# Block numbers loaded four at a time, last stores not held back, and two steps of a hand-written order moved

## The reference, cut to what matters

```python
def _L0_ffn_ref(hidden_states, gate_weight, gate_up_proj, down_proj):
    NUM_EXPERTS, TOP_K, THRESHOLD, HIDDEN, INTER = 32, 8, 0.8, 256, 96
    x = hidden_states.reshape(-1, H)
    probs = softmax(x @ gate_weight.T)
    top_vals, top_idx = top_k(probs, TOP_K)
    renorm = top_vals / sum(top_vals)
    num_keep = minimum(sum(cumsum(renorm) < THRESHOLD) + 1, TOP_K)
    rw = top_vals * (arange(TOP_K) < num_keep);  rw = rw / sum(rw)
    combine = sum(one_hot(top_idx, NUM_EXPERTS) * rw[..., None], axis=1)
    for w_gu, w_d, ce in experts:          # a scan over the 32 experts
        g, u = split(x @ w_gu.T)
        out += (silu(g) * u) @ w_d.T * ce[:, None]

x = x + attention(layernorm(x))
x = x + cross_attention(layernorm(x), ctx)
x = x + _L0_ffn_ref(layernorm(x), ...)
```

## Time and profile before

| | |
|---|---|
| runs shown | 521.94 us median of 3 (520.2 to 522.55) |
| profiled execution | 522.98 us, its span 521.0 us, mean granted clock 0.97 |
| PE, DVE, POOL, ACT busy | 89%, 73%, 63%, 61% of the span |
| chain that ended last | PE 52%, DVE 18%, DMA 8%, issue 7%, SPq 7%, ACT 6% |

### The profile page before, as it was taken

One profiled execution on the slowest core, in us unless ns is written; L12 is line 12 of the kernel. 1 busy time (PEld: TensorE's weight loads), 2 busy tenths in 40 slices (PEclk: granted clock), 3 DMA queues, 4 the chain that ended last, 5 costly groups with the idle time before them and its releaser, 6 DMA issues.

```text
span 521.0 us, 12667 instructions
## 1 busy us (share of the span) xinstructions
PE 464.8 (89%) x3120; PEld 394.9 (76%) x3120; DVE 379.2 (73%) x1854; ACT 317.7 (61%) x869; POOL 327.0 (63%) x473
## 2 busy tenths in 40 slices
PE   3789999999999999999977999999999999798930
PEld 2577777788787778777757898889999999697820
DVE  4356788888877888887875886556556568988796
ACT  2367778787777777777843565556566565455520
POOL 4112257778777678776667667776676666574770
PEclk9989999999999999999987999999999999999985
DMA  6322446852223223221137569998655679988685
GB/s 196 95 111 75 164 128 211 239 161 91 93 97 103 103 92 115 80 99 72 73 121 227 177 220 297 302 294 281 200 147 162 194 220 336 337 281 311 220 294 182
DMA packets 52263, 93.80 MB, mean 180 GB/s; under 512 B 9975, under 2 KB 41247, under 8 KB 52003
## 3 DMA queue, kind: packets, MB, share of 16 engines
q1 hardware_dynamic: 37346, 46.11, 30.4%
q0 software_dynamic: 12240, 32.14, 16.5%
q10 hardware_dynamic: 2608, 14.76, 8.3%
HBM read 53.61 MB, written 43.41 MB: 186 GB/s over the span
## 4 chain that ended last, share of the span: by engine, by line
PE 52%; DVE 18%; DMA 8%; issue 7%; SPq 7%; ACT 6%; POOL 1%; POOLq 0%; ACTq 0%; DVEq 0%
PE bank L1406 11%; PE bank L1441 7%; DVE NM L788 6%; PE bank L1103 6%; PE bank L1244 4%; DVE NM L790 4%; PE bank L1361 4%; PE bank L1286 3%; SPq L360 3%; PE bank L1260 3%; DMA pool_a<-rows 3%; DMA qN<-rows 2%; SPq L365 2%; PE bank L1165 2%; PE bank L1431 2%
## 5 line engine op out<-in xcount | busy, mean ns | idle before, releaser
L468 POOL DMA_INDIRECT rows<-rowb,idx x112 | 110.8, 989 | 56.7 <-DVE rowb L888 28.3
L1406 PE MATMUL bank<-wgu_sb,PT 128*128 x572 | 108.6, 333 | 3.2 <-issue 3.2
L1406 PEld LDWEIGHTS bank<-wgu_sb,PT 128*128 128x128 f32 x572 | 93.3, 194 | 4.8 <-issue 4.4
L478 POOL DMA_INDIRECT parts<-PT,dst_all x72 | 71.5, 993 | 33.1 <-issue 23.8
L495 ACT ACTIVATE PT<-bank 128x512 f32<-128x512 f32 x108 | 61.2, 593 | 29.7 <-PE bank L1441 21.2
L1441 PE MATMUL bank<-wd_sb,VC 96*128 x286 | 75.0, 384 | 1.8 <-issue 1.3
L997 DVE SCALAR_TENSOR_TENSOR PT<-PT,bank 128x192 f32<-128x192 f32 x72 | 25.2, 350 | 53.4 <-ACT PT L622 53.4
L1441 PEld LDWEIGHTS bank<-wd_sb,VC 96*128 96x128 f32 x286 | 51.3, 189 | 9.8 <-issue 5.6
L588 ACT ACTIVATE PT<-bank 128x512 f32<-128x512 f32 x96 | 53.6, 619 | 4.6 <-PE bank L1260 4.5
L622 ACT ACTIVATE PT<-bank 128x192 f32<-128x192 f32 x72 | 23.8, 330 | 50.4 <-PE bank L1406 50.4
L495 ACT ACTIVATE Q<-bank 9x256 fp32r<-9x256 f32 (+1 forms) x96 | 42.5, 443 | 11.3 <-PE bank L1239 9.6
(11 more groups left out here) (270 smaller groups left out, 1148.7 us busy)
## 6 DMA issues: line engine op xcount, KB each, us to landing
pool_a<-rows SPq DMA_DIRECT2D x96, 148.5 KB
qN<-rows SPq DMA_DIRECT2D x47, 148.5 KB
wgu_sb<-wgu_d SPq DMA_DIRECT2D x8, 768.0 KB, 5.2
rows<-pad SPq DMA_DIRECT2D x33, 152.0 KB
pool_a<-parts ACTq DMA_DIRECT2D x5, 896.0 KB
KA<-parts ACTq DMA_DIRECT2D x5, 896.0 KB, 6.8
Q<-parts ACTq DMA_DIRECT2D x5, 896.0 KB
wd_sb<-wd_d SPq DMA_DIRECT2D x2, 1536.0 KB, 10.7
```

The costliest lines, as they stand in the source:

```text
L468: gp.indirect_dma_start(out=rows, out_offset=bass.IndirectOffsetOnAxis(ap=idx[b % 2][:, k:k + 1], axis=0), in_=rowb[b % 2][:, :], in_offse ...
L478: gp.indirect_dma_start(out=parts, out_offset=bass.IndirectOffsetOnAxis(ap=dst[q % NDST][:, j:j + 1], axis=0), in_=yb[q % FEED][:, j, :], ...
L1406: last = t.matmul(GU_PS[q % 2][:, j * 2 * NI:(j + 1) * 2 * NI], xTb[q % 2][:, j, k * P:(k + 1) * P], wgu_sb[:, k, one_of(expert[i]), :].sq ...
```

## The change

1. `choose` takes a pair instead of a pair and a block. For every second pair it loads four numbers into four registers (`pe.load`) and keeps each (`pe.snap`); before, each block had its own `value_load`. The 143 loads become 36. Their place moves from behind each block's gate and up product to the end of the down product of the pair before.
2. The second stores of pairs 48 to 67 no longer wait for `th`.
3. POOL's inverse root of the last tile gets sort key 48.4 instead of 51.3.
4. `la3` gets 87.8 instead of 86.2 on PE, and 88.2 instead of 86.5 on DVE.

```diff
+CLOSE = 48
-           "la2": 80 + (SEEN - 1) * PERIOD, "la3": 86.2 + (SEEN - 1) * PERIOD},
+           "la2": 80 + (SEEN - 1) * PERIOD, "la3": 87.8 + (SEEN - 1) * PERIOD},
...
-    "POOL": {"r17": 28.5, "wo": 51.3}}
+    "POOL": {"r17": 28.5, "wo": 48.4}}
...
-                    if j == 1 and DEEP <= q < NPAIR - 4:
+                    if j == 1 and DEEP <= q < CLOSE:
                         pool.wait_ge(S["th"], nth("th", q + 4))
...
+            four = [pe.alloc_register(f"expert{n}") for n in range(4)]
...
-            def choose(q, j):
-                i = 2 * q + j
-                if i == NA:
+            def choose(q):
+                if q >= NPAIR or q % 2:
+                    return
+                if 2 * q == NA:
                     pe.wait_ge(S["lists"], 4)
-                expert[i] = pe.value_load(tbl_i[0:1, i:i + 1], min_val=0, max_val=NE - 1)
+                pe.load(four, tbl_i[0:1, 2 * q:2 * q + 4])
+                for n in range(4):
+                    expert[2 * q + n] = pe.snap(four[n], min_val=0, max_val=NE - 1)
...
             def gates(q):
-                for j in range(2):
-                    if q < NPAIR and j < BLOCKS[q]:
-                        gu(q, j)
-                    if q + 1 < NPAIR and j < BLOCKS[q + 1]:
-                        choose(q + 1, j)
+                for j in range(BLOCKS[q] if q < NPAIR else 0):
+                    gu(q, j)
...
-                for q in range(2):
-                    for j in range(2):
-                        choose(q, j)
+                choose(0)
                 gu(0, 0)
                 gu(0, 1)
...
                     if q > 0:
                         dn(q - 1)
+                    choose(q + 2)
                     hT_(q)
...
                     gates(q + 2)
                     dn(q - 1)
+                    choose(q + 3)
```

More of the change, by code:

```diff
@@ L65 @@
            "po": 62.9, "g7": 64, "g8": 73.7, "g9": 74.2, "g10": 75.2, "g11": 75.4, "g12": 75.6, "g13": 75.8, "la1": 77.4 + (SEEN - 1) * PERIOD,
-           "la2": 83 + (SEEN - 1) * PERIOD, "la3": 86.5 + (SEEN - 1) * PERIOD},
+           "la2": 83 + (SEEN - 1) * PERIOD, "la3": 88.2 + (SEEN - 1) * PERIOD},
     "POOL": {"r1": -12, "r4": -2.2, "r7": 3.9, "r13": 17.4, "kL": 29.5, "r17": 46.3, "wo": 51.5, "xT": 60, "sc0": 74.6, "sc1": 77.4, "sc2": 80.5,
```

## The result

The changed kernel takes 513.93 us in the median of 4 runs (512.39 to 516.68). The kernel before, run beside it, takes 522.25. The ratio is 0.9846, 95% interval 0.9808 to 0.9885. The medians are 8.3 us apart; the forecast was 514.6 us, 7.3 less than before. The profiled execution took 512.39, span 510.5, mean granted clock 0.983 (before 522.98, 521.0, 0.97).

A forecast was written before the change was run, and what follows sets the result against it. PE bounds 346 to 424 us; the waits lie before and after. 4.4 - 0.8 + 0.8 + 0.5 + 2.9 - 0.5 + 0 = 7.3 us off 522.98 gives 515.7, as median 514.6; range 511.5 to 519.3, forecast's own 513 to 517.

The forecast's parts named there:

- First use, idle: PE at the list's first use: one load replaces four, first gate product 2.2 us earlier, bounds 1.9 to 2.5.
- The clock: PE behind the first use of the list: stays at 2.4 GHz after the shorter idle, 3.0 us gained, bounds 0 to 3.0.
- The root: POOL at the last tile: the move alone gives nothing; in the old place about 3 of 4.4 us would go.
- POOL's queue: POOL's scatters and stores after the head: delay DVE before pair 13, losing 1.0 to 2.7 us; 0.8 taken off.
- Loads in the pairs: PE after waits for rows: fewer loads give 0.8 us before 346 us and 0.5 later, bounds 0 to 2.5.
- Stores not held: Last stretch: POOL keeps up, last store 3.9 us earlier, gain 2.9 at the end; 0.5 off for delayed rows.
- The tail's sum: The end: 2.9 us gained, from 1.0, 0.2 of DVE's 0.83 and its 1.67 wait for the last fetch.
- The list's product: PE ahead of the list's product: waits for DVE's maxima either way, zero gain, bounds -0.3 to +0.5 us.
- The clock did not fall: Rival at the list's first use: the clock falls all the same, 516.9 us, chance 0.16.
- POOL's queue took nothing that reached the end: Rival: POOL's queue takes the head's gain, its 2.00 us idle at 305.46 stays, 517.3 us, chance 0.14.
- no row was crowded out: Rival after 430 us: stores crowd out rows, 10.4 us lost against 7.3 gained, 525.0 us, chance 0.12.
- The change does nothing at the end: Rival at the end: rows or sums, not stores, set DVE; tail gives 0.5, not 2.9; 517.0 us, chance 0.06.

The follow-up runs named there:

- three more edits: Changed kernel with ten destination buffers, the first list's product as before, and ACT's last copy ahead of tile 13's fetch: 513.26 us, 0.9825 of the kernel before.

## Why the prediction was right

The time, the sign and the forecast's own range (513 to 517) hold. By its steps:

- **First use, idle.** Forecast 2.2, measured 2.2 (2.94 to 0.75), since ACT's copy is late next. The load of four took 336 ns in the median. The Trainium skill, "Runtime: NRT & Kernel Launch", section "Instruction fetch mechanics", has 200 ns per register even in bulk, for loads from HBM. The trace doesn't agree for this table: 336 ns for four registers.
- **The clock.** Forecast that it stays full, for 3.0 us. It stayed in all 11 profiles with the short idle. But the 3.0 is a price of one execution: with the long idle it fell for 6.8 us, for 3.4 us and not at all in three profiles (pair 0 at 24.9, 24.0 and 21.8). The profile that the forecast was read from is the one with the longest fall, and that this size fits the medians is in part luck. Undoing the first use's load on top of the pairs' costs 2.9 us, give or take 2.6 (0.9979 - 0.9924): the idle's 2.2, and 0.7 for the rest.
- **The root.** Forecast: by itself nothing, without it 3 of 4.4 would go. The mechanism is shown on both sides: with the loads as before the new place, the list and the stores not held give 0.9979 together. The size was 4.5; in its profile the clock falls behind the wait that the old place leaves, 5.1 us by pair 4.
- **POOL's queue.** DVE's wait for pair 5's store grew from 1.64 to 2.76 us and ended at 316.88, which is 318.7 by the clock of the profile before; forecast was near 320. That it takes 0.8 us from the end isn't shown: with the waits gone, the time was the same. From pair 4 to pair 20 the lead did not fall (5.4 to 5.7).
- **Loads in the pairs.** Forecast 0.8 ahead of 346 us and 0.5 behind. This term was mis-sized: 3.2 us in all, and of that some 1.6 behind pair 16. I had counted five places and taken off what rows or DVE hide; in one profile five gaps of 1.75 us in all stand against a loss of 1.6.
- **Stores not held.** Forecast 2.9 less 0.5. The step that failed is "POOL idles 3.92 us for `th`", and with it "without the hold POOL keeps up". Only about 1.4 of the 3.92 us were the hold; the other 2.5 have another cause, which still makes a gap without the hold (3.05 us in place of 1.28), and the stores of pair 61 come 1.0 to 1.8 us closer, where the forecast had the last store 3.9 us earlier. Behind it POOL runs without a gap from 471.59 to 497.31, as it did before from 482.32. These are 20 stores and 19 steps, not 21 stores at 25.65 / 20 = 1.28: 25.72 / 19 is 1.35 us each, and before 25.65 / 19 was as much. Against PE's 1.41 a block that leaves little to catch up with. At the end PE is faster than that: its last five transposes of the gated product are 2.5 us apart (478.71 to 488.77), since the last pairs have no transposes of new rows and no gate products, and POOL needs 2.7 for two stores. ACT's 2.01 us for a landing fell to 0.8 to 0.9. The last down product ends near 490.5, 6.8 us ahead of the last store, and so it was before (near 501.2). Measured for the hold: 0.7 to 1.4 us.
- **The tail's sum** came out (3.1 us in the profile, 2.9 forecast), which is luck: the two last errors cancel, loads too small by 1, hold too large by 1 to 2. Neither size is resolved by the runs, and in single profiles with the changed kernel's code behind pair 53 the tail runs from 74.4 to 78.1.
- **The list's product**: zero, as forecast.
- **The rivals.** The clock did not fall; POOL's queue took nothing that reached the end; no row was crowded out, and the Trainium skill's rule that each DMA engine takes packets from its queues in turn ("DMA: Bandwidth & Descriptors", "Queues, rings and completion order") went with a mild outcome: 3.2 us of waits for rows, before 3.7. The turns themselves no run here shows. "The change does nothing at the end" was half right, for the stores.

The parts don't add up: undone one at a time they cost 6.4 (loads), 4.5 (root), 0 (list) and about 1 us (hold), 12 in all for a gain of 7.5 (1 - 0.9856). Loads and root share theirs: without the loads 1.1 us of the gain are left (1 - 0.9979), without the root's move 3.0 (1 - 0.9942).

## What to carry to other kernels

Of two waits in a row, removing one is worth what the next one leaves: an early product needed an early root, and an early root with a late product only made another queue wait. The register loads of the engine that sets the time were hidden while that engine had a lead, and showed as 0.2 to 0.5 us after a wait; count the waits, not the share of busy time. Before a wait is priced, hold its end against the end of what the program waits for there, and against the same wait one pair earlier: 0.77 us behind the tanh at pair 60, and 3.30 at pair 61, says that something else holds the store. A queue's own rate at the very end, where the producer has less to do for each block, decides when its last store goes.

## What was not expected of the hardware

- **Behind the same idle the clock fell in one execution and not in the next.** In the 14 profiles PE stands still 1.6 to 1.8 us once, ahead of a product that starts between 261 and 266 us. In 8 the clock then falls to 0.50, in 6 it stays at 1.00, in one and the same kernel too (the changed one: 1.00, 1.00, 0.50). It is low for 3.4 us in seven of them, and in the six of these with the short idle at the first use pair 0 comes at 20.1 to 20.2 all the same; in the kernel with three more edits it was low for 6.8 us, and pair 0 came 1.3 us late. What decides between the two was not tried.
- **A gap of POOL that nothing releases.** Between the two stores of pair 61 pass 3.05 us in place of 1.28, to the hundredth, in all eleven profiles without the hold (468.54 to 471.59 in the first of the changed kernel, 466.27 to 469.32 in the second). With the hold, in the other three, the second of them comes 3.30 us behind its tanh in place of 0.77. The profile names DVE in seven of the eleven, ACT in three and nothing in one, and without the hold the program has no wait between the two stores of a pair. Up to there POOL stores a pair 1.4 us after ACT's copy of it (467.17 and 468.54), two pairs later 2.6 us (472.82 and 475.45), and it doesn't catch up. So part of what holds the last store is this gap and no wait of the program. What makes it was not tried; the DMA queues that the trace calls "instruction" move nothing between the two stores in any of the 14 profiles, so a fetch of instructions that lands there isn't seen.
